# Two transpose banks shared in rotation, and every third weight load moved to SyncE's queue, in an eight-core attention and ternary-FFN kernel

## The chip, the cores and the metric

One Trainium2 chip, all eight NeuronCores. Each core runs the same program on one of the eight sequences of the batch, and no core waits for another. The metric is the device time of the slowest core in microseconds (us). The engines are called PE (TensorE, matmuls), DVE (VectorE), ACT (ScalarE), POOL (GpSimd) and SP (SyncE, which here only issues DMAs).

## The reference

One post-norm transformer layer on x of shape (8, 2048, 2048), cut to what is computed:

```python
q, k, v = x @ Wq, x @ Wk, x @ Wv            # 32 query heads, 8 key/value heads of 64; rope on q, k
a = softmax(causal(q k^T / 8)) v            # heads joined again
x = layernorm(x + a @ Wo)                   # no affine part
def weight_quant(w):                        # ternary: one scale for the whole matrix
    s = 1 / clip(mean(abs(w)), 1e-5); return clip(round(w * s), -1, 1) / s
def bitlinear(x, w):                        # w: (out, in)
    return quant8(rmsnorm(x)) @ weight_quant(w).T
h = silu(bitlinear(x, w_gate)) * bitlinear(x, w_up)       # hidden 8192
x = layernorm(x + bitlinear(h, w_down))
```

The biases are zero but added. `mean(abs(w))` needs one pass over each of the three weight matrices (64 MB each in fp32) before any of them can be quantised.

## The kernel before, in words

The program is written as a list of steps. `S.add(engine, channel, key, fn, deps)` appends a step to one engine's program; the order of the calls is the order on that engine, and a step waits (on semaphores) for every step in `deps`. An engine runs its steps strictly in that order. A DMA step belongs to the engine whose queue issues it, and its wait holds up whatever stands behind it on that engine. Each channel has one semaphore and belongs to one engine. `Rot` hands out buffers in rotation: `next()` gives the slot, the buffer and what last used it (`fr`), `used()` records who must be done before the slot comes round again.

The stages, in order:

- **x and its transposes** (0 to 358 us). For each of 16 token tiles `m`: SP loads x (1 MB, two buffers, `axl`), ACT casts it to bf16 (`axc`, L299), PE transposes it into psX, four blocks of 128 columns at a time, and DVE copies each out (`axe`, L315; 4 of them). Then 8 **pieces** of the weight-mean pass.
- **The weight-mean pass**, `pp_piece`. 384 pieces of 128x1024 fp32 (512 KB). A piece is a load (`ppl`, L285) into one of three buffers `pp_stg`, issued by ACT, and a sum of absolute values on DVE (`ppa`, L287). 128 pieces stand in the first stage, 8 for each m; 256 stand in the attention stage, 4 for each head pair. Piece `idx` uses slot `idx % 3`.
- **q, k, v** (to 1256 us). Weights come in 256 KB pieces through SP (`awl`, L328) and are cast by ACT (L332).
- **Attention** (to about 4500 us). Four query blocks g of 512, in each 16 head pairs p. For a pair: scores on PE and exp on ACT for all key tiles (`bexp`, L542), then the four pieces (their loads stand on ACT's queue behind the pair's last exp, their sums on DVE in front of the pair's `bave`), then for both heads: psAV (L560), its copy av_s (`bave`, L569), transposes, the division and the copy into attn_fm. PE starts the next pair's scores only after that, so exp waits for the whole chain. Then the output projection with 2 MB slabs through SP, and the norms.
- **FFN part 1** (about 4500 to 8640 us). First the activations come back and are transposed: 16 tiles, in each two groups of eight 128x128 transposes (`fxt`, L828) into **one** PSUM bank psTT, each copied out by DVE (`fxe`, L835). Then 64 blocks `ht` of 128 hidden rows. In a block DVE quantises the gate rows to ternary (terng, L855 to L858) and the up rows (ternu, L864 to L867). PE transposes each in two groups of eight (`ftt`, L879) through the same psTT, and DVE copies each group out (`fte`, L886) to wgT or wuT. Then for n = 0..3: 16 matmuls gate (L893), 16 matmuls up (L916), DVE's products, a max and a min, and a small matmul of the squares (L944). At the end of the block DVE quantises 128x2048 of w_down (L969 to L972), PE transposes it in two groups through another single bank psTD (`fdt`, L981), DVE copies both out (`fde`, L988), and POOL stores them.
- **FFN part 2** (to the end): int8 activations, the down projection, the last norm. Nothing in it is touched.

The chains that keep one bank from being overwritten are two variables: `last_tt` holds the last copy out of psTT and `last_fde` that out of psTD, and each next group of transposes depends on it.

DVE's order in a block is: terng, ternu, copy g0, copy g1, copy u0, copy u1, then the products of n = 0..3, then ternd, copy d0, copy d1. PE's is: transposes g0, g1, u0, u1, the matmuls of n = 0..3, transposes d0, d1.

Of the kernel before, what the change touches and what calls it, by code (L numbers as in the profile page):

```python
# [9 lines left out]
BF16 = mybir.dt.bfloat16  # L10
# [141 lines left out]
def build(nc, debug=(), upto="ALL"):  # L152
# [40 lines left out]
    S = Sched(nc, top)  # L193
# [79 lines left out]
    def pp_piece(idx):  # L273
# [10 lines left out]
        S.add("scalar", pp_stg.ch(sl), ("ppl", idx),  # L284
# [126 lines left out]
    for i in range(64):  # L411
        r, c = divmod(i, 4)
# [345 lines left out]
    psTT = ps(fst, "psTT", [128, 1024], BF16)  # L758
    psTD = ps(fst, "psTD", [128, 1024], BF16)
# [57 lines left out]
    last_tt = [None]  # L817
    xq_sp_done = [S.last("d_xqs0"), S.last("d_xqs1")]
    for m in range(NT):
# [5 lines left out]
        for j in range(2):  # L825
            def xtf(e, b=buf, j=j):
                for c in range(8 * j, 8 * j + 8):
                    i = e.transpose(psTT[:, (c % 8) * 128:(c % 8 + 1) * 128],  # L828
                                    b[:, c * 128:(c + 1) * 128], identb[:])
                return i  # L830
            S.add("tensor", "mm", ("fxt", m, j), xtf, deps=[("fxl", m), last_tt[0]])
            def xte(e, m=m, j=j):
                dst = xqT[:].rearrange("p (f t) -> p f t", f=ND)[:, 8 * j:8 * j + 8,
                                                                m * 128:(m + 1) * 128]
                return e.tensor_copy(dst, psTT[:].rearrange("p (s c) -> p s c", s=8))  # L835
            S.add("vector", "ve", ("fxe", m, j), xte, deps=[("fxt", m, j)])
            last_tt[0] = ("fxe", m, j)
# [4 lines left out]
    last_fde = [None]  # L842
    for ht in range(NFH):
# [30 lines left out]
        for nm, tern, dstT, dfr, qkey in (("g", terng, gT, gTfr, ("fgq", ht)),  # L874
                                          ("u", ternu, uT, uTfr, ("fuq", ht))):
            for j in range(2):
                def ttf2(e, tern=tern, j=j):
                    for c in range(8 * j, 8 * j + 8):
                        i = e.transpose(psTT[:, (c % 8) * 128:(c % 8 + 1) * 128],  # L879
# [3 lines left out]
                      deps=[qkey, last_tt[0]] + (dfr if j == 0 else []))  # L883
                def tte(e, dstT=dstT, j=j):
                    dst = dstT[:].rearrange("p (f c) -> p f c", f=ND)[:, 8 * j:8 * j + 8, :]
                    return e.tensor_copy(dst, psTT[:].rearrange("p (s c) -> p s c", s=8))  # L886
                S.add("vector", "ve", ("fte", nm, ht, j), tte, deps=[("ftt", nm, ht, j)])
                last_tt[0] = ("fte", nm, ht, j)
# [89 lines left out]
        for j in range(2):  # L978
            def dtf(e, o=tdb, j=j):
                for c in range(8 * j, 8 * j + 8):  # L980
                    i = e.transpose(psTD[:, (c % 8) * 128:(c % 8 + 1) * 128],  # L981
# [3 lines left out]
                  deps=[("fdq", ht), last_fde[0]] + (wtfr if j == 0 else []))  # L985
            def dte(e, wtb=wtb, j=j):
                dst = wtb[:].rearrange("p (c q) -> p c q", c=ND)[:, 8 * j:8 * j + 8, :]
                return e.tensor_copy(dst, psTD[:].rearrange("p (s c) -> p s c", s=8))  # L988
            S.add("vector", "ve", ("fde", ht, j), dte, deps=[("fdt", ht, j)])
            last_fde[0] = ("fde", ht, j)  # L990
# [12 lines left out]
    for n in range(4):  # L1003
        po = (n % 2) * 64
        for c in range(4):
            idx = n * 4 + c
            S.add("tensor", "mm", ("fstt", idx),
                  lambda e, po=po, n=n, c=c, idx=idx: e.transpose(
                      psTT[:, (idx % 8) * 128:(idx % 8) * 128 + 64],
                      stp[po:po + 64, (n // 2) * 512 + c * 128:(n // 2) * 512 + (c + 1) * 128],  # L1010
                      identb[po:po + 64, po:po + 64]),
                  deps=[("fsv",), ("fstr", idx - 1) if idx >= 1 else None,
# [265 lines left out]
```

How the kernel before makes its waits and increments, by code:

```python
    def bar(self, e, inst):  # L82
        ch = self._cur_ch
        self.ecnt[ch] = self.ecnt.get(ch, 0) + 1
        inst.then_inc(self.sem(ch), 1)
        e.wait_ge(self.sem(ch), self.ecnt[ch])
# [17 lines left out]
            def body(eng):  # L104
                waited = {}
                for s in engsteps:
                    own = ENGCH.get(s.eng)
                    ownv = self.ecnt.get(own, 0) if own is not None else 0
                    if own is not None and ownv > waited.get(own, -1):
                        eng.wait_ge(self.sem(own), ownv)
                        waited[own] = ownv
                    for d in s.deps:
                        ch, v, peng = table[d]
                        if waited.get(ch, -1) >= v:
                            continue
                        eng.wait_ge(self.sem(ch), v)
                        waited[ch] = v
                    self._cur_ch = s.ch
                    inst = s.fn(eng)
                    inst.then_inc(self.sem(s.ch), s.inc)
                    self.ecnt[s.ch] = self.ecnt.get(s.ch, 0) + s.inc
                    assert self.ecnt[s.ch] == table[s.key][1], \
                        f"step {s.key}: emitted {self.ecnt[s.ch]} != planned {table[s.key][1]} (nbar mismatch)"
```

## Time and profile before

| | |
|---|---|
| median of 3 runs | 11738.02 us (11729.38 to 11750.48) |
| the profiled execution | 11751.26 us, span of its slowest core (core 3) 11749.7 us |
| spans of the eight cores | 11715.5 to 11749.7 us |
| mean granted TensorE clock | 0.701 to 0.706 of full speed |
| busy: PE / DVE / ACT / POOL | 5747.7 / 4763.7 / 1243.3 / 955.1 us |
| idle time of DVE before L287, ended by a landing pp_stg load | w_down 851.6, w_up 477.3, w_gate 111.9 us |

Busy time is a mean over stages with different limits. PE is busy for 49% of the span, DVE for 41%, so neither is the bound throughout: what sets the time in each stage is a chain that goes from one engine to the other and back. The text after the number in square brackets on a row of the timeline says what ended the idle time before that instruction.

### The profile page before, as it was taken

What the parts mean: (1) busy time and instruction counts of PE and PEld (TensorE: products, weight loads), DVE (VectorE), ACT (ScalarE), POOL (GpSimd) and SP (SyncE); (2) the same over time, 40 slices, a digit from 0 to 9 for tenths busy, and PEclk for the clock granted to TensorE, in tenths of its full rate; (3) what the DMA queues carried; (4) which work ended last, traced back from release to release, by engine and by line L of the source; (5) the groups of instructions that cost most, each with busy time, mean ns of one, the idle gap of its engine ahead of it and who ended that gap; (6) DMA issues with size and microseconds to landing.
All of it is one profiled execution on the core that took longest, in us unless ns stands there. A gap on an engine that the chain in (4) does not pass through costs nothing. (4 is left out here: it accounts for less than half of the span.)

```text
span 11749.7 us, 84716 instructions; the slowest of 8 cores (11715.5 to 11749.7 us)
## 1 busy us (share of the span) xinstructions
PE 5747.7 (49%) x27032; PEld 2847.2 (24%) x27032; DVE 4763.7 (41%) x6288; ACT 1243.3 (11%) x2029; POOL 955.1 (8%) x1158
## 2 busy tenths in 40 slices
PE   1463243545545663656656666665630455303554
PEld 0221111111111121222222222222210344202443
DVE  5440234242242125444444444444445333464333
ACT  0101111213313420000000000000000000000000
POOL 0000110101100100000000000000013000031000
PEclk9876555565565565777777877877765778656877
DMA  7423231121121122222222222222212111122111
GB/s 237 138 82 88 80 97 61 65 83 54 50 84 46 43 77 74 79 79 75 74 79 80 68 79 79 73 75 79 76 49 72 49 52 37 64 73 60 38 51 50
DMA packets 394188, 865.55 MB, mean 74 GB/s; under 512 B 33140, under 2 KB 234004, under 8 KB 363030
## 3 DMA queue, kind: packets, MB, share of 16 engines
q1 hardware_dynamic: 286424, 482.57, 13.2%
q10 hardware_dynamic: 64512, 218.13, 5.9%
q0 software_dynamic: 42816, 159.43, 4.0%
q8 instruction: 225, 3.69, 0.1%
q14 instruction: 211, 1.73, 0.1%
HBM read 700.62 MB, written 159.40 MB: 73 GB/s over the span
## 5 line engine op out<-in xcount | busy, mean ns | idle before, releaser
L1164 PE MATMUL psD<-wdts,xcol 128*128 128x256 bf16 x8192 | 1152.3, 313 | 1841.7 <-DVE xcol L1155 1603.8
L1164 PEld LDWEIGHTS psD<-wdts,xcol 128*128 128x128 bf16 x8192 | 908.2, 112 | 2087.1 <-issue 1875.2
L893 PE MATMUL psG<-xqT,wgT 128*128 128x512 bf16 x4096 | 1105.0, 431 | 0.0
L287 DVE TENSOR_REDUCE ppart<-pp_stg 128x1 f32<-128x1024 f32 x384 | 468.5, 1220 | 1471.6 <-DMA pp_stg<-w_down 851.6
L916 PE MATMUL psU<-xqT,wuT 128*128 128x512 bf16 x4096 | 925.8, 379 | 0.0
L528 PE MATMUL psS<-qT,kT 64*128 64x512 bf16 x1280 | 653.8, 578 | 200.8 <-ACT pA L542 109.3
L1178 DVE SCALAR_TENSOR_TENSOR z2h<-psD,c3col,x2c 128x256 bf16<-128x256 f32 x128 | 61.9, 484 | 1357.5 <-PE psD L1164 1357.5
L901 DVE TENSOR_TENSOR gtr<-psG,gbc 128x512 f32<-128x512 f32 x256 | 177.0, 692 | 1004.3 <-PE psG L893 1004.3
L893 PEld LDWEIGHTS psG<-xqT,wgT 128*128 128x128 bf16 x4096 | 429.0, 109 | 600.8 <-issue 277.9
L1155 DVE CAST xcol<-xq2res 128x8192 bf16<-128x8192 int8 x128 | 566.7, 4427 | 13.6 <-DVE z2h L1178 0.5
L542 ACT ACTIVATE pA<-psS 128x512 bf16<-128x512 f32 x640 | 382.1, 597 | 1443.8 <-PE psS L528 1356.1
L916 PEld LDWEIGHTS psU<-xqT,wuT 128*128 128x128 bf16 x4096 | 400.8, 98 | 483.3
L352 PE MATMUL psQ<-wslab,xT 128*128 128x512 bf16 x1536 | 420.9, 447 | 184.9 <-ACT wslab L332 184.9
L906 ACT ACTIVATE gsil<-gtr 128x512 f32<-128x512 f32 x256 | 161.1, 629 | 2886.3 <-DVE gtr L901 2886.3
L879 PE MATMUL psTT<-identb,terng 128*128 128x128 bf16 x1024 | 129.5, 307 | 602.8 <-DVE terng L858 362.6
L952 POOL DMA_DIRECT2D h_spill<-h2c x256 | 139.1, 543 | 3281.6 <-DVE h2c L924 3167.8
L542 ACT ACTIVATE pB<-psS 128x512 bf16<-128x512 f32 x640 | 382.2, 597 | 96.5 <-ACT pA L542 3.8
L1128 POOL TENSOR_TENSOR tq<-h2rl,cbc 128x1024 f32<-128x1024 f32 x128 | 299.3, 2338 | 656.1 <-DVE xq2res L1139 622.7
L560 PE MATMUL psAV<-pA,v_buf 128*65 128x512 bf16 x640 | 256.2, 578 | 176.2 <-POOL pA L547 176.2
L574 PE MATMUL psW<-identf,av_s 65*128 65x65 f32 x512 | 77.0, 296 | 538.7 <-DVE av_s L569 538.7
L944 PE MATMUL psST<-sqc,onesb 128*64 128x512 bf16 x256 | 96.5, 377 | 475.6 <-ACT sqc L940 475.6
L547 POOL TENSOR_SCALAR_AFFINE_SELECT pA<-pA 128x512 bf16<-128x512 bf16 x256 | 156.7, 612 | 2059.4 <-ACT pA L542 2022.6
(178 smaller groups left out, 6371.4 us busy)
## 6 DMA issues: line engine op xcount, KB each, us to landing
pp_stg<-w_gate ACTq DMA_DIRECT2D x128, 512.0 KB, 5.6
pp_stg<-w_up ACTq DMA_DIRECT2D x128, 512.0 KB, 4.8
pp_stg<-w_down ACTq DMA_DIRECT2D x128, 512.0 KB, 4.6
wgst<-w_gate SPq DMA_DIRECT2D x64, 1024.0 KB, 5.0
wust<-w_up SPq DMA_DIRECT2D x64, 1024.0 KB, 4.8
wdst<-w_down SPq DMA_DIRECT2D x64, 1024.0 KB, 4.8
h_spill<-h2c POOLq DMA_DIRECT2D x256, 256.0 KB, 2.6
h2rl<-h_spill SPq DMA_DIRECT2D x128, 512.0 KB, 3.6
```

Of the source, the lines that this page charges most:

```text
L287: lambda e, b=buf, idx=idx: e.tensor_reduce(ppart[:, idx:idx + 1], b[:], AX.X, OP.add, apply_absolute_value=True),
L352: i = e.matmul(p_[:], xT[:, kc * T + m * 128:kc * T + (m + 1) * 128], w[:, kc * 512:(kc + 1) * 512], start=(kc == 0), stop=(kc == 15))
L528: lambda e, kv=kv, kt=kt, p=p, poff=poff, bank=bank: e.matmul(psS[bank][:], kT[poff:poff + 64, kv * T + kt * 128:kv * T + (kt + 1) * 128], ...
L542: lambda e, pb=pX[X], kt=kt, bank=bank: e.activation(pb[:, kt * 512:(kt + 1) * 512], psS[bank][:], AF.Exp),
L560: i = e.matmul(psAV[0:65, :], v_buf[:, kt * 520 + hv * 65:kt * 520 + hv * 65 + 65], pb[:, kt * 512:(kt + 1) * 512], start=(kt == 0), stop= ...
L893: i = e.matmul(p_[:], gT[:, kc * 128:(kc + 1) * 128], xqT[:, kc * T + n * 512:kc * T + n * 512 + 512], start=(kc == 0), stop=(kc == 15))
L901: lambda e, p_=gps, n=n: e.tensor_tensor(gtr[:], p_[:], gbc[:, n * 512:(n + 1) * 512], OP.mult),
L906: lambda e, o=gsb3: e.activation(o[:], gtr[:], AF.Silu),
L916: i = e.matmul(p_[:], uT[:, kc * 128:(kc + 1) * 128], xqT[:, kc * T + n * 512:kc * T + n * 512 + 512], start=(kc == 0), stop=(kc == 15))
L1128: lambda e, b=buf, o=tb, hf=hf: e.tensor_tensor(o[:], b[:], cbc[:, hf * 1024:(hf + 1) * 1024], OP.mult),
L1155: lambda e, o=cb4, m=m: e.tensor_copy(o[:].rearrange("p (k c) -> p k c", k=NFH), xq2res[:].rearrange("p (k c) -> p k c", k=NFH)[:, :, m * ...
L1164: i = e.matmul(p_[0:128, 0:256], c_[:, hk * 128:(hk + 1) * 128], w[:, hk * 256:(hk + 1) * 256], start=(hk == 0), stop=(hk == NFH - 1))
```

## The change

Two things. In the weight-mean pass, the loads of slot 1 are issued by SP in place of ACT (one in three). In FFN part 1, psTT and psTD become one rotation psTX of two banks, and every group of eight transposes (xq, gate, up, down, and the 16 small ones of the sums of squares) takes the next bank and waits only for the copy that last read that bank. The number of PSUM banks, the transposes, the copies and the order on each engine stay as they are, except for the moved loads.

```diff
         sl, buf, fr = pp_stg.next()
-        S.add("scalar", pp_stg.ch(sl), ("ppl", idx),
+        S.add("scalar" if sl != 1 else "sync", pp_stg.ch(sl), ("ppl", idx),
               lambda e, b=buf, s=src: e.dma_start(out=b[:], in_=s), deps=[fr], dma=True)
...
-    psTT = ps(fst, "psTT", [128, 1024], BF16)
-    psTD = ps(fst, "psTD", [128, 1024], BF16)
+    psTX = Rot([ps(fst, f"psTX{i}", [128, 1024], BF16) for i in range(2)], "psTX")
...
         for j in range(2):
-            def xtf(e, b=buf, j=j):
+            tsl, tbuf, tfr = psTX.next()
+            def xtf(e, b=buf, j=j, tb=tbuf):
...
-            S.add("tensor", "mm", ("fxt", m, j), xtf, deps=[("fxl", m), last_tt[0]])
+            S.add("tensor", "mm", ("fxt", m, j), xtf, deps=[("fxl", m)] + tfr)
...
             S.add("vector", "ve", ("fxe", m, j), xte, deps=[("fxt", m, j)])
-            last_tt[0] = ("fxe", m, j)
+            psTX.used(tsl, ("fxe", m, j))
...
                 S.add("tensor", "mm", ("ftt", nm, ht, j), ttf2,
-                      deps=[qkey, last_tt[0]] + (dfr if j == 0 else []))
+                      deps=[qkey] + tfr + (dfr if j == 0 else []))
...
                 S.add("vector", "ve", ("fte", nm, ht, j), tte, deps=[("ftt", nm, ht, j)])
-                last_tt[0] = ("fte", nm, ht, j)
+                psTX.used(tsl, ("fte", nm, ht, j))
...
             S.add("tensor", "mm", ("fdt", ht, j), dtf,
-                  deps=[("fdq", ht), last_fde[0]] + (wtfr if j == 0 else []))
+                  deps=[("fdq", ht)] + tfr + (wtfr if j == 0 else []))
...
             S.add("vector", "ve", ("fde", ht, j), dte, deps=[("fdt", ht, j)])
-            last_fde[0] = ("fde", ht, j)
+            psTX.used(tsl, ("fde", ht, j))
...
-                  deps=[("fsv",), ("fstr", idx - 1) if idx >= 1 else None,
-                        ("fte", "u", NFH - 1, 1)])
+                  deps=[("fsv",), ("fte", "u", NFH - 1, 1)] + tfr)
```

## Rows read from the trace of the kernel before

**Rows 1.** Stretches: time, busy PE, PEld, DVE, ACT, POOL, PEclk, DMA, GB/s.

```profile
1256.00:4500.00 3244.00, 1592.79 (x5024) 542.56 (x5024) 1055.91 (x2315) 780.68 (x1318) 328.85 (x541) 0.58 0.20 66
4640.00:8640.00 4000.00, 2448.28 (x11524) 1151.69 (x11524) 1919.20 (x2246) 323.69 (x513) 245.46 (x320) 0.79 0.23 75
```

**Rows 2.** Timeline, one FFN block, gate and up weights: start, duration, instruction, idle before.

```profile
6451.81 1.23 DVE L858 TENSOR_TENSOR terng<-pq_b,qq_b 128x2048 bf16<-128x2048 bf16 x1
...
6453.28 1.01 PE L879 MATMUL psTT<-identb,terng 128*128 128x128 bf16 x8 [5.62 <-DVE terng L858]
...
6457.19 0.69 DVE L886 COPY wgT<-psTT 128x1024 bf16<-128x1024 bf16 x1 [0.17 <-DVE ternu L867]
6458.03 1.01 PE L879 MATMUL psTT<-identb,terng 128*128 128x128 bf16 x8 [3.73 <-DVE wgT L886]
6459.14 0.69 DVE L886 COPY wgT<-psTT 128x1024 bf16<-128x1024 bf16 x1 [1.26 <-PE psTT L879]
6460.09 1.01 PE L879 MATMUL psTT<-identb,ternu 128*128 128x128 bf16 x8 [1.05 <-DVE wgT L886]
...
6462.04 1.01 PE L879 MATMUL psTT<-identb,ternu 128*128 128x128 bf16 x8 [0.94 <-DVE wuT L886]
6462.85 4.92 PE L893 MATMUL psG<-xqT,wgT 128*128 128x512 bf16 x16
...
6512.69 1.22 DVE L858 TENSOR_TENSOR terng<-pq_b,qq_b 128x2048 bf16<-128x2048 bf16 x1
```

**Rows 3.** Timeline, the same block's w_down transposes.

```profile
6444.69 1.01 PE L981 MATMUL psTD<-identb,ternd 128*128 128x128 bf16 x8 [4.42 <-DVE ternd L972]
6445.81 0.69 DVE L988 COPY wdtst<-psTD 128x1024 bf16<-128x1024 bf16 x1 [1.37 <-PE psTD L981]
6446.65 1.01 PE L981 MATMUL psTD<-identb,ternd 128*128 128x128 bf16 x8 [0.94 <-DVE wdtst L988]
6447.76 0.69 DVE L988 COPY wdtst<-psTD 128x1024 bf16<-128x1024 bf16 x1 [1.26 <-PE psTD L981]
```

**Rows 4.** Instructions of tile terng: count, duration min/median/max ns, first and last start.

```profile
L858 DVE TENSOR_TENSOR terng<-pq_b,qq_b x64: 1224/1225/1227, 4644.7 to 8576.1; 128x2048 bf16<-128x2048 bf16 x64
```

**Rows 5.** Stretches of one or a few us inside FFN blocks, columns as in rows 1.

```profile
6462.80:6465.20 2.40, 2.40 (x9) 0.93 (x7) 0.69 (x1) 0.00 (x0) 0.00 (x0) 0.50 0.00 0
...
6421.00:6424.50 3.50, 3.50 (x10) 1.23 (x9) 0.00 (x0) 0.00 (x0) 0.00 (x0) 0.52 0.01 4
```

**Rows 6.** Timeline, gate matmuls of two successive n in one block.

```profile
6410.76 3.63 PE L893 MATMUL psG<-xqT,wgT 128*128 128x512 bf16 x16
...
6420.05 5.31 PE L893 MATMUL psG<-xqT,wgT 128*128 128x512 bf16 x16
```

**Rows 7.** Timeline, one of the 32 xq transpose groups.

```profile
4580.62 1.01 PE L828 MATMUL psTT<-identb,xqrl 128*128 128x128 bf16 x8 [0.94 <-DVE xqT L835]
```

**Rows 8.** Tile xqrl: landing times of its 16 loads.

```profile
DMA to landing us min/median/max: 3.3/3.8/12.6
```

**Rows 9.** Timeline, attention, one head pair whose first piece is in slot 1.

```profile
1404.54 5.78 ACTq L285 DMA_DIRECT2D pp_stg<-w_up  x4
...
1408.68 1.22 DVE L287 TENSOR_REDUCE ppart<-pp_stg 128x1 f32<-128x1024 f32 x1 [10.19 <-DMA pp_stg<-w_up]
...
1414.13 1.22 DVE L287 TENSOR_REDUCE ppart<-pp_stg 128x1 f32<-128x1024 f32 x1 [1.44 <-DMA pp_stg<-w_up]
1415.52 0.69 DVE L569 COPY av_s<-psAV 65x512 f32<-65x512 f32 x1 [0.17 <-DVE ppart L287]
```

**Rows 10.** Timeline, first stage, end of tile m = 9 and start of m = 10.

```profile
228.56 1.22 DVE L287 TENSOR_REDUCE ppart<-pp_stg 128x1 f32<-128x1024 f32 x1 [0.17 <-DVE ppart L287]
...
230.35 1.91 ACT L299 ACTIVATE xbf<-x_stage 128x2048 bf16<-128x2048 f32 x1 [20.58 <-DVE ppart L287]
...
237.34 0.42 DVE L315 COPY xT<-psX 128x512 bf16<-128x512 bf16 x1 [0.17 <-DVE ppart L287]
```

**Rows 11.** Tile x_stage: landing times of its 16 loads.

```profile
DMA to landing us min/median/max: 7.0/8.1/10.0
```

More of the change, by code:

```diff
@@ L876, in build, with ttf2 @@
             for j in range(2):
-                def ttf2(e, tern=tern, j=j):
+                tsl, tbuf, tfr = psTX.next()
+                def ttf2(e, tern=tern, j=j, tb=tbuf):
                     for c in range(8 * j, 8 * j + 8):
-                        i = e.transpose(psTT[:, (c % 8) * 128:(c % 8 + 1) * 128],
+                        i = e.transpose(tb[:, (c % 8) * 128:(c % 8 + 1) * 128],
                                         tern[:, c * 128:(c + 1) * 128], identb[:])
@@ L978, in build, with dtf @@
         for j in range(2):
-            def dtf(e, o=tdb, j=j):
+            tsl, tbuf, tfr = psTX.next()
+            def dtf(e, o=tdb, j=j, tb=tbuf):
                 for c in range(8 * j, 8 * j + 8):
-                    i = e.transpose(psTD[:, (c % 8) * 128:(c % 8 + 1) * 128],
+                    i = e.transpose(tb[:, (c % 8) * 128:(c % 8 + 1) * 128],
                                     o[:, c * 128:(c + 1) * 128], identb[:])
@@ L1006, in build @@
             idx = n * 4 + c
+            tsl, tbuf, tfr = psTX.next()
             S.add("tensor", "mm", ("fstt", idx),
-                  lambda e, po=po, n=n, c=c, idx=idx: e.transpose(
-                      psTT[:, (idx % 8) * 128:(idx % 8) * 128 + 64],
+                  lambda e, po=po, n=n, c=c, tb=tbuf: e.transpose(
+                      tb[:, 0:64],
                       stp[po:po + 64, (n // 2) * 512 + c * 128:(n // 2) * 512 + (c + 1) * 128],
                       identb[po:po + 64, po:po + 64]),
-                  deps=[("fsv",), ("fstr", idx - 1) if idx >= 1 else None,
-                        ("fte", "u", NFH - 1, 1)])
+                  deps=[("fsv",), ("fte", "u", NFH - 1, 1)] + tfr)
             S.add("vector", "ve", ("fstr", idx),
-                  lambda e, idx=idx: e.tensor_reduce(
-                      ftm[:, idx:idx + 1], psTT[:, (idx % 8) * 128:(idx % 8) * 128 + 64],
+                  lambda e, idx=idx, tb=tbuf: e.tensor_reduce(
+                      ftm[:, idx:idx + 1], tb[:, 0:64],
                       AX.X, OP.add),
                   deps=[("fstt", idx)])
+            psTX.used(tsl, ("fstr", idx))
     fam_last = [("famP", NFH - 1, 3), ("famN", NFH - 1, 3)]
```

16 lines of the change are left out of this document (7 added, 9 removed).

## The prediction, as it went on record

> **What bounds the kernel now.** I read the list of stretches first, to see which stages the change touches and what they are worth. FFN part 1 takes 4000 us from 4640 on, with PE busy 2448 of them and DVE 1919; the attention stage takes 3244 us with PE busy 1593, DVE 1056 and ACT 781 [rows 1]. No engine is full in either, so a chain from engine to engine sets the time, and the timeline has to say which.
>
> In an FFN block the timeline [rows 2] shows where PE is idle before the matmuls. The gate rows are ternary at 6453.04 and the first gate matmul starts at 6462.85, 9.81 us later. In between PE works 4 times 1.01 us. It waits for ternu, because DVE makes ternu before it copies out the first group; then each group waits for the copy of the one before, and each copy for its group. DVE is idle 1.26 us before each of the copies after the first. Here the two engines take turns in one bank. The same turn-taking stands at the end of the block [rows 3], and there it is DVE's own chain: the next block's terng is queued behind the second wdtst copy. The block lasts 60.88 us from terng to terng [rows 2]; over all 64 the mean is (8576.1 - 4644.7)/63 = 62.40 us [rows 4].
>
> In the attention stage the four sums of a head pair stand in front of av_s on DVE. Their loads are issued behind the pair's last exp: from the first issue to av_s it is 10.98 us in the pair shown [rows 9]. Everything behind av_s, up to the next pair's exp, waits. In the first stage the last of each tile's loads holds ACT's cast of the next x tile, which is then already in its buffer [rows 10].
>
> **The change part by part, FFN.** Nothing is added to an engine; two waits for a bank go away in each pair of groups. The rotation is g0, g1, u0, u1, d0, d1 in banks 0, 1, 0, 1, 0, 1, so a group waits for the copy two places earlier. For g0 and d0 these copies are long done.
>
> *Gate and up.* g0 runs at 6453.28 as before and g1 directly behind it, both under ternu. DVE copies g0 at 6457.19 to 6457.88 as before, then g1 at 6458.05 to 6458.74 (0.17 between DVE steps, as in front of the copy at 6457.19). PE's u0 can start 0.15 after the first copy, at 6458.03, where g1 stood. u1 follows it: behind eight transposes at 0.81 us a group (6462.04 to 6462.85), but not before 6458.74 + 0.15 = 6458.89. The gate matmuls start at 6458.89 + 0.81 = 6459.70 in place of 6462.85, which is 3.15 us earlier. The copies of u0 and u1 end near 6460.8, under the gate matmuls, before the up matmuls need them.
>
> *Down.* d1 follows d0 at 6445.50 and ends at 6446.51; the second copy starts at 6446.50 + 0.17 = 6446.67 and ends at 6447.36 in place of 6448.45, 1.09 us earlier, and terng of the next block moves with it.
>
> Sum: 4.24 us a block, 64 blocks: 271 us. Between the two places PE's and DVE's matmul part is unchanged.
>
> *Clock.* The first part of the gate matmuls runs at 0.50, which is 1.2 GHz [rows 5], so they take 4.92 us [rows 2] against 3.63 [rows 6]. PE's unbroken work begins at 6462.04, 0.81 us before the gate matmuls; after the change it begins at 6458.03, 1.67 us before them. If the clock rises as long after its beginning as now, 0.86 us less of the matmuls is at half speed, 0.43 us a block, 27 us in all; if it doesn't, nothing. I take 20. The clock also falls inside some blocks: 0.52 over 3.5 us [rows 5], which makes 16 matmuls 5.31 us long instead of 3.63, 1.68 more [rows 6]. Such stretches, and the varying first part, are what lifts the mean block over the shown one: 62.40 - 60.88 = 1.52 us, 97 us over 64 blocks. Where they fall depends on how the block's pattern lies in time, which the change shifts. They may all go (97 gained) or double (97 lost). I take zero, as the part of the block in which they fall is unchanged.
>
> *xq transposes.* A group takes 1.01 + 0.94 = 1.95 us [rows 7]; with two banks each bank is reused after 1.95, so 0.98 a group, 31 us over 32 groups. But both groups of a tile wait for its load, and there are two load buffers: a buffer's load can't be issued before its tile is transposed and lands 3.3 to 3.8 us later [rows 8], so a tile takes 3.4 to 3.9 us after the change against 3.91 now. That leaves 0 to 8 us. With the 16 small transposes at the end I take 5 and keep 0 to 35.
>
> FFN in all: 271 + 20 + 5 = 296 us.
>
> **Attention.** The loads of slot 1 now stand on SP, which in the pairs has nothing else to issue. So slot 1 is filled again as soon as DVE has summed it, long before the pair's last exp. Four pieces on three slots: a pair starts in slot 2, 0 or 1 in turn. In pairs that start in slot 2 or 0 the fourth piece takes the slot of the first; ACT still issues that load only when the first is landed and summed, and av_s stays where it is: gain 0. In pairs that start in slot 1 both slot-1 pieces are already there and summed or landed, ACT issues two loads in place of four, and nothing is issued late. The first landed sum starts 4.14 us after the issue (1408.68 - 1404.54); three sums at 1.39 apart (1415.52 - 1414.13) end the wait at 4.14 + 3 x 1.39 = 8.31 in place of 10.98 [rows 9], a gain of 2.67. I take 2.4, since not every pair waits as long for the fourth load. There are 21 such pairs of 64: 50 us. Bounds: 0 (the loads contend with each other) and 21 x 2.67 with some more where slabs of Wo delay the fourth load, 75.
>
> This is where a page speaks against the change. The trace shows loads of 512 KB whose first sum comes 4.14 us after the issue, whatever the queue is [rows 9]. The Trainium skill, page "DMA: Bandwidth & Descriptors", section "Issuing engines are not separate DMA queues", says that queues of several engines run on the same 16 DMA engines, and that using several saves only the sequencers' time to issue. By that rule the 50 us would be 0. I think that the rule doesn't reach this case, since what is saved is the wait behind exp and not bandwidth.
>
> **First stage.** Here SP isn't free: it loads x. The load of tile m+1 stood ahead, waiting only for a cast that is long done; now it stands behind the slot-1 pieces of tile m, each of which waits for a sum on DVE. Nothing in this stage hides it: DVE's copies of tile m+1 wait for PE, PE for the cast, the cast for x.
>
> - Tiles with slots 0 1 2 0 1 2 0 1 (m = 0, 3, ..., 15): the eighth piece waits for the fifth sum, 229.78 in tile 9 [rows 10]. x is issued at about 230.3 and lands 8.1 us later [rows 11], 238.4; the cast of 1.91 is done at 240.3, and with some 1 us for PE's transposes (a group of eight takes 1.01 [rows 7]) the first copy comes at 241.3 (now the cast could let it come at 233.3, and the sums hold it until 237.34). Late by 3.9 us, five times before the last tile: 20.
> - Tiles with 1 2 0 1 2 0 1 2: the seventh piece waits for the fourth sum, 1.39 us earlier: late by 2.5, five times: 12.
> - Tiles with 2 0 1 ...: the sixth waits for the third sum, early enough for the cast; but 1 MB then moves while DVE waits for its own pieces. I take 1, five times: 5.
> - After the last tile the first Wq pieces, also prefetched by SP now, are issued late: 3, once.
>
> Loss 40 us. With landing at 7.0 and no contention it would be about 20, and 10 if prefetched slot 1 pieces give something back; with 10.0 at each of the 15 tiles 5.8 x 15 = 87.
>
> **Sum.** -296 - 50 + 40 = -306 us. The profiled execution took 11751.26 us, so 11445; the median of the runs shown is 13 us below the profiled one, so 11432 us.
>
> **The rivals.**
>
> *A, the clock takes part of the gain back.* If the half-speed stretches of 3.5 us come in most blocks and the earlier rise doesn't, FFN gives 271 - 97 + 5 = 179 us and the time is 11549. Half of that effect gives about 11500. For it: the clock does fall inside blocks now. Against: the matmul part keeps its pattern.
>
> *B, the lost prefetch of x costs more.* 87 in place of 40: 11479.
>
> *C, attention gains nothing*, as the queue rule has it: 11482.
>
> *D, the FFN gain isn't there, because a second bank doesn't shorten a chain that something else holds.* Then -50 + 40 = -10: 11728, no change that can be told. Against it stand all four idle times in [rows 2] and two in [rows 3], which name the copy or the transposes and nothing else. The Trainium skill, page "TensorE: Matmul & The Clock Gate", section "HAM oscillation — how this bites in real kernels", tells of a kernel in which double-buffering PSUM gave no further gain; by that FFN would give nothing. That kernel waited for loads, and here the rows name no load.
>
> *E, slower.* One mechanism: PE works more densely, and the clock falls in nearly every n of the 256. Each fall costs 1.68 us [rows 6]. To eat 306 us it needs 182 more falls than now; if every n had one more, 430 us would be lost and the time is 11862. For it: only that the falls exist; against: the density inside n is unchanged.
>
> *F, the clock gives more*: the falls go away, and 97 us with them: 11335.
>
> **How the numbers follow.** The forecast has 0.68, A 0.10, B 0.07, C 0.06, F 0.05, D 0.02, E 0.02. The range reaches from 11345 (most of F, with the attention and first-stage terms at their better ends) to 11510 (B and C, half of A). What lies outside is the rest of A and F, D and E, near 0.15. A measurement of this kernel can tell about 0.2%, 23 us, from no change. Only D lies within it and only E above: faster 0.95, same 0.03, slower 0.02.
>
> **What would show it.** In the changed profile: the time from the end of terng to the first gate matmul 6.66 us in place of 9.81; no idle of 0.94 us between transpose groups; 2.67 us from the first w_down transposes to the second wdtst copy's end in place of 3.76; mean block near 57.9. In attention: every third pair with two loads on ACT's queue and av_s 8.2 us after the first issue, the others at 10.4 to 11. In the first stage: the cast waits for x in place of a sum, and the stage ends near 395 in place of 358. FFN part 2 unchanged. The prediction is wrong if FFN blocks get shorter by less than 3 us (the clock), if the pairs of the other two kinds move, or if the first stage doesn't grow.

## The result, and the profile after

The changed kernel takes 11429.53 us (median of 8 runs, 11405.74 to 11447.54), the kernel before 11740.51 (8 runs on the same chip, 11729.38 to 11751.99). The ratio is 0.9735, with a 95% interval of 0.9724 to 0.9745. The forecast was 11432. The profiled execution took 11437.69 us, with a span of 11436.0 on core 3, which is also the core shown of before.

This table lays core 3's two spans side by side, cut at the instructions named. The 5.1 us between the last xq transpose and the first terng stand in no row and are the same in both:

| stretch | before | after | change | predicted |
|---|---|---|---|---|
| start to the end of the 128th L287 | 365.6 | 404.4 | +38.8 | +37 |
| to the first q matmul | 25.3 | 29.2 | +3.9 | +3 |
| q, k, v, to the first score | 869.6 | 875.6 | +6.0 | 0 |
| attention, first score to last av_s | 3074.2 | 3015.9 | -58.3 | -50 |
| to the first xq transpose | 242.0 | 242.1 | +0.1 | 0 |
| xq transposes | 62.9 | 47.3 | -15.6 | -5, with the small ones |
| 63 blocks, terng to terng | 3931.4 | 3654.2 | -277.2 | -286 |
| the last block | 60.3 | 55.6 | -4.7 | -4.6 |
| small transposes and the rest up to psD | 539.1 | 534.2 | -4.9 | in the -5 |
| FFN part 2 | 2574.1 | 2572.3 | -1.8 | 0 |

The changes add up to -313.7 us, for a forecast of -306. The page's row of the sums of absolute values has 816.0 us of idle time ended by w_down's loads where the one before had 851.6:

```profile
L287 DVE TENSOR_REDUCE ppart<-pp_stg 128x1 f32<-128x1024 f32 x384 | 468.5, 1220 | 1437.9 <-DMA pp_stg<-w_down 816.0
```

**FFN part 1.** These are the two stretches that answer to [rows 1], moved to where the stages now lie; the columns are the same.

```profile
1305.00:4500.00 3195.00, 1572.59 (x5024) 536.09 (x5024) 1063.49 (x2330) 780.89 (x1319) 329.39 (x542) 0.59 0.21 67
4620.00:8330.00 3710.00, 2400.86 (x11520) 1164.03 (x11520) 1912.95 (x2239) 323.70 (x513) 244.30 (x320) 0.81 0.25 81
```

FFN part 1 needs 3710 us for the DVE work for which it needed 4000 (1912.95 us against 1919.20), so what went is DVE's idle time. The timeline of one block, from the w_down transposes of the block before to the gate matmuls, answers to [rows 2, 3]:

```profile
6643.64 1.87 PE L981 MATMUL psTX<-identb,ternd 128*128 128x128 bf16 x16 [4.42 <-DVE ternd L971]
6644.76 0.69 DVE L988 COPY wdtst<-psTX 128x1024 bf16<-128x1024 bf16 x1 [1.37 <-PE psTX L981]
6645.62 0.69 DVE L988 COPY wdtst<-psTX 128x1024 bf16<-128x1024 bf16 x1 [0.17 <-PE psTX L981]
...
6649.66 1.23 DVE L856 TENSOR_TENSOR terng<-pq_b,qq_b 128x2048 bf16<-128x2048 bf16 x1
...
6651.14 1.86 PE L878 MATMUL psTX<-identb,terng 128*128 128x128 bf16 x16 [5.64 <-DVE terng L856]
...
6655.05 0.69 DVE L885 COPY wgT<-psTX 128x1024 bf16<-128x1024 bf16 x1 [0.17 <-DVE ternu L865]
6655.91 0.69 DVE L885 COPY wgT<-psTX 128x1024 bf16<-128x1024 bf16 x1 [0.17 <-DVE wgT L885]
...
6655.99 1.87 PE L878 MATMUL psTX<-identb,ternu 128*128 128x128 bf16 x16 [2.98 <-DVE wgT L885]
6657.10 0.69 DVE L885 COPY wuT<-psTX 128x1024 bf16<-128x1024 bf16 x1 [0.51 <-PE psTX L878]
...
6657.65 5.15 PE L892 MATMUL psG<-xqT,wgT 128*128 128x512 bf16 x16
```

Sixteen transposes now stand in one row where there were two groups of eight with 0.94 idle between them. From terng's end (6650.89) to the first gate matmul it is 6.76 us. In the w_down part, first transposes to the end of the second copy (6646.31) is 2.67 us. All 64 blocks are in the row of terng, which answers to [rows 4]: the mean block is (8273.9 - 4619.6)/63 = 58.00 us.

```profile
L856 DVE TENSOR_TENSOR terng<-pq_b,qq_b x64: 1224/1225/1227, 4619.6 to 8273.9; 128x2048 bf16<-128x2048 bf16 x64
```

The clock still falls inside blocks, as in [rows 5, 6]. Here are PE instructions of the same block, the second and the third gate row, each behind a small matmul (L943). The stretch below them lies in the third gate row and has the granted clock 0.52:

```profile
6668.05 0.38 PE L943 MATMUL psST<-sqc,onesb 128*64 128x512 bf16 x1 [1.79 <-ACT sqc L939]
6668.35 3.63 PE L892 MATMUL psG<-xqT,wgT 128*128 128x512 bf16 x16
...
6677.34 0.38 PE L943 MATMUL psST<-sqc,onesb 128*64 128x512 bf16 x1 [1.90 <-ACT sqc L939]
6677.65 5.31 PE L892 MATMUL psG<-xqT,wgT 128*128 128x512 bf16 x16
```

```profile
6677.90:6681.40 3.50, 3.50 (x10) 1.31 (x9) 0.00 (x0) 0.00 (x0) 0.00 (x0) 0.52 0.22 80
```

**Attention.** A pair that starts in slot 1, in the timeline (answers to [rows 9]):

```profile
3976.15 0.82 ACTq L285 DMA_DIRECT2D pp_stg<-w_down  x2
...
3980.16 1.22 DVE L287 TENSOR_REDUCE ppart<-pp_stg 128x1 f32<-128x1024 f32 x1 [26.30 <-DMA pp_stg<-w_down]
3981.55 1.22 DVE L287 TENSOR_REDUCE ppart<-pp_stg 128x1 f32<-128x1024 f32 x1 [0.17 <-DVE ppart L287]
3982.95 1.22 DVE L287 TENSOR_REDUCE ppart<-pp_stg 128x1 f32<-128x1024 f32 x1 [0.17 <-DVE ppart L287]
3984.24 0.33 SPq L285 DMA_DIRECT2D pp_stg<-w_down  x1
3984.34 0.69 DVE L569 COPY av_s<-psAV 65x512 f32<-65x512 f32 x1 [0.17 <-DVE ppart L287]
```

ACT issues two loads and av_s starts 8.19 us after the first. The prediction says of these loads' time that it is the same "whatever the queue is", for which [rows 9], with ACT's loads alone, was no evidence. The changed kernel has it: a load that SP issues with no other piece in flight lands after 3.67 us (median of 362 in all cores), and one that it issues some 1.4 us behind one of ACT's after 4.70. In the kernel with all loads on ACT's queue further down (*the middle key tile*) the same two figures are 3.69 and 4.70.

**First stage.** The end of tile m = 9 and the start of m = 10 (answers to [rows 10]), and the landing times of x_stage ([rows 11]):

```profile
251.39 0.38 SPq L295 DMA_DIRECT2D x_stage<-x  x1
...
258.18 0.33 SPq L285 DMA_DIRECT2D pp_stg<-w_gate  x1
259.29 1.91 ACT L299 ACTIVATE xbf<-x_stage 128x2048 bf16<-128x2048 f32 x1 [23.58 <-DMA x_stage<-x]
...
262.14 0.42 DVE L315 COPY xT<-psX 128x512 bf16<-128x512 bf16 x1 [4.04 <-PE psX L307]
```

```profile
DMA to landing us min/median/max: 6.2/8.1/11.2
```

ACT's cast is now released by x itself, where a sum released it before, and DVE is idle for 4.04 us in front of the first copy. The forecast had 3.9 us late for such a tile. Tiles 1, 4, 7, 10 and 13 have 4.1 to 4.4 us of it (means of the cores), tiles 3, 6, 9, 12 and 15 have 0.8 to 1.0, and the others 0.2, as every tile had before.

### The profile page after: what moved, and what is told of

Read it like the earlier page. It is cut to its first block and busy times, and to the rows that moved or that the text cites. A ratio compares the mean times of both kernels' runs of the same rounds, so it can differ in the third digit from the quotient of the medians.

```text
span 11436.0 us, 84644 instructions; the slowest of 8 cores (11383.3 to 11436.0 us)
## 1 busy us (share of the span) xinstructions
PE 5682.2 (50%) x27032; PEld 2855.3 (25%) x27032; DVE 4763.7 (42%) x6288; ACT 1243.3 (11%) x2029; POOL 955.1 (8%) x1158
## 3 DMA queue, kind: packets, MB, share of 16 engines
q8 instruction: 225, 3.69, 0.1%
## 5 line engine op out<-in xcount | busy, mean ns | idle before, releaser
L287 DVE TENSOR_REDUCE ppart<-pp_stg 128x1 f32<-128x1024 f32 x384 | 468.5, 1220 | 1437.9 <-DMA pp_stg<-w_down 816.0
L943 PE MATMUL psST<-sqc,onesb 128*64 128x512 bf16 x256 | 96.9, 379 | 475.5 <-ACT sqc L939 475.5
L923 DVE TENSOR_TENSOR h2c<-psU,gsil 128x512 f32<-128x512 f32 x256 | 177.1, 692 | 319.4 <-PE psU L915 319.2
```

The costliest lines, as they stand in the source:

```text
L287: lambda e, b=buf, idx=idx: e.tensor_reduce(ppart[:, idx:idx + 1], b[:], AX.X, OP.add, apply_absolute_value=True),
L923: lambda e, p_=ups, o=h2b, g_=gsb3: e.tensor_tensor(o[:], p_[:], g_[:], OP.mult),
```

## The experiments

Each batch had its own runs of the kernel before; their medians were 11765.41 (first batch), 11774.21 (second) and 11741.65 us (third). Stage and block times are those of core 3 unless a range over cores is given.

Totals are compared by their ratios, and with one more caution. The total is that of the slowest core, and in all runs but one some cores have stretches at a granted clock of 0.81 in FFN part 1 (last section), not the same ones each time. In *slot 1 early* core 5, the slowest, had 532 us of it there and a mean block of 59.34 us, where the cores without it had 58.0: 83 us in the total that the edit didn't make. In *banks only* core 7 had 309 us and 58.78, which is 48. So the readings below go by stages, and by the blocks of cores that had little or none of it.

### The two halves apart

*Banks only*: the rotation of two banks, all piece loads on ACT.

```diff
-        S.add("scalar" if sl != 1 else "sync", pp_stg.ch(sl), ("ppl", idx),
+        S.add("scalar", pp_stg.ch(sl), ("ppl", idx),
```

> The two banks in rotation, with all weight loads issued by ACT as in the kernel before. Theory: the shift in the FFN stage and nothing else, 277 us in the 63 blocks between the first and the last terng, 5 in the last block, 16 in the xq transposes, 5 in the small transposes at the end: about 304 us under the kernel before, so near 11437 us, a ratio of 0.974. The stage up to the last L287 of the 128th piece ends at 365.6 as before, and attention (first scores to last av_s) takes 3074 us as before. Rival 1: the moved loads carry part of the gain, in that the FFN stage gains less without them; then the 63 blocks keep more than 3700 us. Rival 2: a second bank gives nothing; ratio 1.00.

Measured 11488.57 us, ratio 0.975 (0.9707 to 0.9793); the expected 11437 lacks the 48 us at 0.81. First stage 365.1, attention 3068.8, mean block 58.02.

*Queue only*: the kernel before, with slot 1's loads on SP (the same line the other way round).

> Only the slot-1 loads moved to SP, psTT and psTD as in the kernel before. Theory: first stage 39 us longer, first Wq pieces and the q, k, v stage up to 10 us longer, attention 58 us shorter: a net of -10 to -20 us, 11720 to 11730 us, a ratio of 0.998 to 0.999. Blocks at 62.40 us. Rival (queues of several engines share the same DMA engines, so that nothing is gained by a second queue): attention stays at 3074 us and the kernel is 40 us slower, ratio 1.003.

Measured 11747.84 us, ratio 0.9979 (0.9958 to 0.9999). First stage 403.1, attention 3000.9, mean block 62.42.

The halves don't touch each other: each has its own stages' times of the changed kernel and the other half's times of before. The banks make all of the FFN gain. The queue alone is worth about 25 us by its ratio, with an interval of 1 to 49: some 70 gained in attention, some 40 lost in the first stage and 6 more up to the first q matmul.

### Was the loss in the first stage x's place behind the pieces?

*x ahead*: SP loads tile m+1 before it comes to tile m's pieces.

```diff
+    x_next = x_load(0)
     for m in range(NT):
+        sl, buf = x_next
+        if m + 1 < NT:
+            x_next = x_load(m + 1)
```

> The changed kernel, with x tile m+1 issued on SP's queue before tile m's slot-1 pieces. Theory (x lost its place in the queue): first stage back from 404 us to about 366, Wq pieces still late by up to 4, total about 11391 us, a ratio of 0.970 to the kernel before. Rival (x and a third of the pieces now share SP's rings and slow each other down, whatever the order): first stage stays above 390 and the total at 11430. Second rival: with x ahead and a second queue, the pieces themselves come earlier, first stage under 355.

Measured 11431.07 us, ratio 0.9705 (0.9671 to 0.974). That is 40 us above the expected 11391. On the slowest core 31 of them are blocks at 0.81 (217 us of it, mean block 58.49). The first stage lasts 362 to 383 us over the cores, against 396 to 405. This is the timeline of its m = 9 to 10:

```profile
240.69 1.91 ACT L305 ACTIVATE xbf<-x_stage 128x2048 bf16<-128x2048 f32 x1 [22.16 <-DVE ppart L287]
242.00 0.38 SPq L295 DMA_DIRECT2D x_stage<-x  x1
...
250.07 0.42 DVE L321 COPY xT<-psX 128x512 bf16<-128x512 bf16 x1 [0.17 <-DVE ppart L287]
```

The cast's releaser is a sum again, and DVE goes from its last sum straight to the copy. The mean of the cores is 371.6 us here, 402.5 in *queue only* and 368.2 in *banks only*, all of this batch: 31 of 34 us come back. What was lost has two parts. DVE's idle time in front of the copies of x was 43.0 us before, 66.5 in the changed kernel and is 43.0 again. Its idle time in front of the sums was 116.5 us before, 134.0 in the changed kernel, and is 127.9 here against 124.6 in *banks only*. The first Wq pieces stay late: the stretch to the first q matmul was 32 to 39 us here, 25 to 28 in *banks only*.

### Is it the queue, or the place in the order?

The queue rule of the prediction's rival C says that another queue gives nothing. These two keep every load on ACT and move only where slot 1's loads stand in ACT's order: the first one ahead of the pair's exps, and a pair's second one (if it has two) ahead of the last key tile's exps, or of the middle one's.

```diff
+                if kt == 0:
+                    pp_piece(ones[0], add=False)
+                if kt == nkt - 1 and len(ones) == 2:
+                    pp_piece(ones[1], add=False)
```

The other kernel has `kt == nkt // 2` in place of `kt == nkt - 1`. The first to run was the one with the last key tile (*slot 1 early*):

> All piece loads on ACT, but in attention the slot-1 loads stand ahead of the pair's exps (the second one of a pair, where there are two, ahead of the last key tile's exps). No second queue. Theory (the place in the program's order, not the queue): attention as in the changed kernel, about 3000 us against 3070 before, first stage as before, about 360, total near 11390. Rival (a second queue is what helps): attention stays at 3060 to 3075 as with the banks alone.

Measured 11481.45 us, ratio 0.9748 (0.9694 to 0.9802); attention 3033 to 3060 us over the cores. The mean of the cores is 3044, against 3067 before and 2996 in the changed kernel, so two thirds of the expected gain are missing. The timeline of a slot-1 pair, whose last exp starts at 3944.01 and takes 0.60:

```profile
3942.83 0.34 ACTq L287 DMA_DIRECT2D pp_stg<-w_down  x1
...
3950.11 1.22 DVE L291 TENSOR_REDUCE ppart<-pp_stg 128x1 f32<-128x1024 f32 x1 [28.09 <-DMA pp_stg<-w_down]
...
3954.29 0.69 DVE L578 COPY av_s<-psAV 65x512 f32<-65x512 f32 x1 [0.17 <-DVE ppart L291]
```

ACT issues its two other loads at 3944.96, and the first sum starts 5.15 us later instead of 4.01 (3980.16 - 3976.15 in the changed kernel). The first of these two lands after 5.42 us (median over such pairs and all cores), where it takes 3.88 in the changed kernel. The load issued 2.1 us ahead of it is then still on its way. So the place in the order isn't all that counts: a load issued while another is on its way lands later, here as above (4.70 us against 3.67).

With the middle key tile in place of the last:

> As the run with slot-1 loads early on ACT, but the second slot-1 load of a pair stands ahead of the exps of the middle key tile in place of the last. In that run the load issued 1.8 us before the last exp's end moved while ACT's own two loads were in flight, and these landed at 5.4 to 6.2 us in place of 3.8 to 4.1. Theory (place and contention, not the queue): pairs that start in slot 1 reach av_s 8.0 to 8.9 us after the last exp in query blocks 1 to 3, as with SP, and attention on core 3 takes 3000 to 3025 us. Rival (a second queue is what helps): these pairs stay at 9.7 us or more and attention at 3045 and above.

Measured 11386.73 us, ratio 0.9702 (0.9681 to 0.9723); attention 2989 to 3004 us. A slot-1 pair in its timeline:

```profile
3886.27 8.50 ACTq L287 DMA_DIRECT2D pp_stg<-w_down  x3
...
3890.35 1.22 DVE L291 TENSOR_REDUCE ppart<-pp_stg 128x1 f32<-128x1024 f32 x1 [27.02 <-DMA pp_stg<-w_down]
...
3894.53 0.69 DVE L578 COPY av_s<-psAV 65x512 f32<-65x512 f32 x1 [0.17 <-DVE ppart L291]
```

First issue to av_s is 8.26 us, as on SP. The first of ACT's two late loads lands after 3.90 us. So the whole attention gain can be had on one queue. The rule of the Trainium skill (page "DMA: Bandwidth & Descriptors", section "Issuing engines are not separate DMA queues"), that a second issuing engine saves only the time to issue, holds here: 2989 to 3004 us with one queue against 2983 to 3016 with two. What paid was to take a load out from behind the exps. And since SP is left alone, x keeps its prefetch: the first stage is back at 352 to 367 us.

*All of attention's pieces on SP*, the first stage's all on ACT: the same idea taken to its end.

```diff
-        S.add("scalar" if sl != 1 else "sync", pp_stg.ch(sl), ("ppl", idx),
+        S.add("scalar" if idx < 128 else "sync",
+              pp_stg.ch(sl) if idx < 128 else f"d_pq{sl}", ("ppl", idx),
```

> The changed banks; the first stage's piece loads all on ACT, the attention stage's all on SP (three slots). Theory (what costs is that a load stands behind the pair's last exp, and in the first stage that x stands behind pieces): first stage back at 355 to 375 us. In attention all four pieces of a pair are loaded and summed during its exps, so av_s starts when PE has finished psAV, 2.2, 4.0, 5.0 and 6.2 us after the last exp in the four query blocks in place of 10.4: (8.2 + 6.4 + 5.4 + 4.2) x 16 = 387 us under the kernel before, so attention near 2685 us and the total near 11060. Rival (the loads' own bandwidth or latency sets the pace, whatever the place of the issue): attention stays above 2900.

Measured 11046.82 us, ratio 0.9384 (0.9337 to 0.9431); attention 2615 to 2649 us over the cores. DVE in one pair of core 4:

```profile
2503.16 1.22 DVE L287 TENSOR_REDUCE ppart<-pp_stg 128x1 f32<-128x1024 f32 x1 [0.17 <-DVE ppart L287]
2506.32 1.22 DVE L287 TENSOR_REDUCE ppart<-pp_stg 128x1 f32<-128x1024 f32 x1 [1.93 <-DMA pp_stg<-w_down]
2523.81 0.69 DVE L569 COPY av_s<-psAV 65x512 f32<-65x512 f32 x1 [16.27 <-PE psAV L560]
```

All sums are done during the pair's exps, and av_s waits for its own matmuls. From the last exp's end to av_s it is 2.5, 4.2, 5.2 and 6.5 us in the four query blocks (medians), against 8.2 to 11.6 in the changed kernel.

### Does the clock take part of the FFN gain back?

*Down in turns*: d1 waits for the copy of d0 again, so 1.09 us a block should come back.

```diff
-                  deps=[("fdq", ht)] + tfr + (wtfr if j == 0 else []))
+                  deps=[("fdq", ht)] + tfr + (wtfr if j == 0 else [("fde", ht, 0)]))
```

> The changed kernel, where the second group of w_down transposes of a block waits again for the copy of the first. Theory: each block loses the 1.09 us that this place was worth, 64 x 1.09 = 70 us: about 11500 us, mean block 59.1 in place of 58.00. Rival: DVE's chain there is bound by something else (the clock, the copies themselves), and the wait costs less than 0.5 us a block, under 11465. Rival 2: the clock's pattern answers to the shift by more than the step itself, and the mean block comes out outside 58.8 to 59.4.

Measured 11459.45 us, ratio 0.9736 (0.9701 to 0.977). The wait is there (PE in its timeline), and yet the mean block is (8227.8 - 4562.0)/63 = 58.19 us, 0.19 above the changed kernel's:

```profile
6647.21 1.01 PE L981 MATMUL psTX<-identb,ternd 128*128 128x128 bf16 x8 [4.39 <-DVE ternd L971]
6649.17 1.01 PE L981 MATMUL psTX<-identb,ternd 128*128 128x128 bf16 x8 [0.94 <-DVE wdtst L988]
```

```profile
L856 DVE TENSOR_TENSOR terng<-pq_b,qq_b x64: 1224/1225/1226, 4562.0 to 8227.8; 128x2048 bf16<-128x2048 bf16 x64
```

I counted the gate and up matmuls of all blocks of core 3 that start 0.43 us after the one before instead of 0.22, which is what a 512-column matmul takes at 1.2 and at 2.4 GHz in these traces. (Core 3 has a record of all 128 of a block. Two cores of each run lack three, and a gap in the records looks like a slow matmul.) In the changed kernel they are 7.1 a block at its beginning and 4.9 later, and the clock falls inside 37 of 63 blocks. With d in turns they are 5.6 and 2.0, and it falls inside 15 to 18. These are 4.4 fewer, each 0.213 us: 0.94 us. So 1.09 were added, 0.94 paid back, which leaves 0.15. The same short waits stood in every block of both kernels, only placed 1.09 us apart; why that makes the falls rarer isn't shown. All eight cores have it, and yet the program alone doesn't fix the count: in the kernel with the middle key tile, whose FFN is the changed kernel's, three cores had 27, 28 and 34.

*Squares late*: the small matmul of the squares (L943), for which PE waits 1.8 to 1.9 us while the gate matmuls behind it could run, stands behind the next n's gate matmuls, for n = 0 to 2.

```diff
         for n in range(4):
...
             S.add("tensor", "mm", ("fgm", ht, n), gmm, ...)
+            if n:
+                late_fsm()
...
-            S.add("tensor", "mm", ("fsm", ht, n), ...)
+            if n == 3:
+                fsm()
+            else:
+                late_fsm = fsm
```

> The changed kernel, with the small matmul of the squares (L944) of n = 0, 1, 2 issued on PE behind the gate matmuls of n + 1. PE no longer idles 1.8 to 1.9 us for ACT's squares in three of four n. Theory of the clock: the clock falls inside a block because of these repeated idle stretches; without them it falls inside at most a tenth of the blocks in place of 37 of 63. Mean block: 58.0 - 3 x 1.8 = 52.6 with the falls as they are, 51.5 without them; total near 11030. Rival (denser work makes the clock fall more often): more than 4.9 matmuls a block at half speed behind the first part, mean block above 53.5.

Measured 11057.53 us, ratio 0.9384 (0.9332 to 0.9437). The clock falls inside none of the 63 blocks, and the mean block is (7845.7 - 4620.2)/63 = 51.20 us. PE in one n:

```profile
6032.88 3.62 PE L892 MATMUL psG<-xqT,wgT 128*128 128x512 bf16 x16
6036.43 0.40 PE L946 MATMUL psST<-sqc,onesb 128*64 128x512 bf16 x1
6036.76 3.63 PE L917 MATMUL psU<-xqT,wuT 128*128 128x512 bf16 x16
```

```profile
L856 DVE TENSOR_TENSOR terng<-pq_b,qq_b x64: 1224/1225/1227, 4620.2 to 7845.7; 128x2048 bf16<-128x2048 bf16 x64
```

Of the 6.80 us a block, three waits of 1.8 to 1.9 us are 5.5; the 4.9 later slow matmuls that are gone are 1.04, and 0.8 fewer at the beginning 0.17. So it was those waits that let the clock fall.

*The same with d in turns*: where there are no falls to take away, the 1.09 us should stay lost.

> The kernel with the squares late (no falls of the clock inside blocks), and the second group of w_down transposes waiting again for the first one's copy. Theory (with the changed kernel the same wait cost only 0.2 us a block, since the clock fell inside 16 blocks in place of 37 and gave back the rest): with no falls to give back, the wait costs its 1.09 us, mean block 52.3 on the cores where it was 51.2, total near 11125. Rival (the wait itself costs little, because the copies on DVE are bound elsewhere): mean block under 51.6.

Measured 11057.96 us, ratio 0.9424 (0.9396 to 0.9452). The mean block is (7852.9 - 4567.4)/63 = 52.15 us, 0.95 above 51.20; the slow matmuls at the beginning went from 6.3 to 5.8, which pays back 0.1. The totals alone could not tell: their ratios are 0.9384 and 0.9424, with intervals that overlap, and the slowest cores had blocks at 0.81 in both runs.

*Filled waits*: the changed kernel with 22 and 10 more matmuls of 128x512 in PE's two long waits of a block, whose results nobody reads.

```diff
+        def keep(key, count, deps):
+            def f(e):
+                for _ in range(count):
+                    i = e.matmul(psG.bufs[0][:], identb[:], xqT[:, 0:512],
+                                 start=True, stop=True)
+                return i
+            S.add("tensor", "mm", key, f, deps=deps)
+        if ht:
+            keep(("kp1", ht), 22, [("fgs", ht - 1, 2)])
...
+            if nm == "u" and ht:
+                keep(("kp2", ht), 10, [])
```

The 22 stand ahead of the gate transposes, the 10 ahead of the up transposes.

> The changed kernel with work that is thrown away: 22 matmuls of 128x512 on PE between a block's w_down transposes and the next block's gate transposes, and 10 between the gate and the up transposes, where PE idles 5.6 and 2.9 us. Theory (the first gate matmuls run at 1.2 GHz since PE idles ahead of them): the 7.1 matmuls a block at half speed go, the gate matmuls of n = 0 take 3.6 us, and the mean block falls by 7.1 x 0.21 = 1.5 us to 56.5: total near 11335. If the falls inside the blocks go too, 55.5 and 11270. Rival (the added matmuls delay the transposes or the clock falls through higher load): mean block 58 or more.

Measured 11351.26 us, ratio 0.9643 (0.9595 to 0.9692). PE in its timeline:

```profile
6614.69 5.52 PE L873 MATMUL psG<-xqT,identb 128*128 128x512 bf16 x22
...
6625.39 0.61 PE L889 MATMUL psTX<-identb,ternu 128*128 128x128 bf16 x8 [1.63 <-DVE wgT L896]
...
6626.59 3.62 PE L903 MATMUL psG<-xqT,wgT 128*128 128x512 bf16 x16
```

The first gate row takes 3.62 us where it took 5.15, and eight transposes 0.61 us where they took 1.01. The mean block falls from 58.00 to 56.84. Two parts make it up (means of the 63 blocks): from the first gate matmul to the first up matmul 4.94 us became 4.17, 0.77 less, and from terng's end to the first gate matmul 6.78 became 6.37, 0.41 less, as the transposes run at the full clock too. The falls inside remain (38 to 46 blocks). In this run the q, k, v stage was also shorter on cores 0 to 3, 821 to 823 us against 850 to 854 on the cores of before that had no granted clock of 0.81 there (see the last section). Its instructions are the same. The difference stands in one place: ACT waits for the 64 pieces of Wo for 205 to 210 us in all, against 227 to 230 before, and these loads land after a median of 2.97 to 3.01 us in place of 3.26 to 3.36 on all eight cores. Why they land sooner is open.

### The pieces together

*Attention's pieces on SP, and squares late:*

> The squares late, and the attention loads all on SP with the first stage's all on ACT. The stages don't touch each other, so the gains add: attention near 2635, blocks at 51.2 to 52.3, first stage 350 to 366: 11047 - 372 = 10675 us, a ratio of 0.907 to 0.910 to the kernel before. Rival (denser work makes the chip grant less clock in the FFN): blocks above 53 on more than two cores and a total above 10740.

Measured 10581.52 us, ratio 0.902 (0.8998 to 0.9041): attention 2616 to 2633 us over the cores, mean block 51.21.

*The same with filled waits:*

> As the run with both, with the thrown-away matmuls (22 and 10 a block) in PE's waits. Gain theory: the 6.3 matmuls at half speed at a block's start fall to about 2, 0.9 us a block, 58 us in all: 10620. Rival (the granted clock falls below full for longer, as cores 4 to 7 showed 0.81 for 807 to 1048 us with the filled waits alone): the stretches at 0.81 exceed 1000 us on some cores, the gate and up matmuls there take 20 percent longer, and the total is 10675 or more.

Measured 10489.41 us, ratio 0.8953 (0.8922 to 0.8984), the fastest kernel of the study. The mean block is 50.38 us in place of 51.21. From the first gate matmul to the first up matmul it is 4.38 us in place of 4.81, and from terng's end to the first gate matmul 6.39 in place of 6.80: 0.43 and 0.41 make up the 0.83. Of the 92 us against the kernel without fillers 52 are the blocks' (63 x 0.83). The q, k, v stage gives some 28 more, and again ACT's wait for Wo's pieces is shorter (204 to 206 us against 226 to 234, landing after 2.95 to 2.98 us against 3.22 to 3.34).

## Why the prediction was right, point by point

The total is closer than its parts. The forecast of 11432 is 2.5 us off, while single terms are off by 9 (the blocks), 8 (attention), 16 (xq and small transposes) and 6 (q, k, v), and most of it cancels: the sum is -313.7 in place of -306, and the median lies 8 us below the profiled run in place of 13. That last closeness is luck.

- **Gate and up: right.** terng's end to the first gate matmul went from 9.82 to 6.76 us, where 6.66 was predicted: 3.06 of the 3.15 us. u1 follows u0 with no wait, since the second wgT copy ends at 6656.60, before u0's eight transposes are through. The missing 0.10: PE starts u0 0.25 us after the first copy's end (6655.74 to 6655.99), and I took 0.15.
- **Down: right.** 3.76 to 2.67 us, as predicted.
- **Clock at the block's beginning: right.** 8.5 slow matmuls became 7.1, 0.30 us a block; 0.31 had been taken.
- **Clock inside the blocks (rival A): right for this kernel.** It falls inside 37 blocks where it fell inside 36. But the reason given, that the matmul part's pattern is unchanged, is weaker than I made it. In the experiment with d in turns the pattern was just as unchanged, and the falls went from 37 blocks to 15 to 18. That the count stayed was partly luck: the kernel could have come out some 40 us (0.62 us x 63 blocks) faster.
- **xq and small transposes: mis-sized.** -15.6 and -4.9 us in place of -5 in all. The step that failed is "a tile takes 3.4 to 3.9 us after the change": the landing (median 3.7 us now, as in [rows 8]) comes once for each two tiles, since two buffers are on their way together. With a tile's two groups of 0.98 us (1.95, [rows 7]) that gives (3.7 + 1.95)/2 = 2.8 us a tile, and the stage took 47.3/16 = 2.96. The whole is inside the bound of 35.
- **Attention: right in kind.** Every third pair went from 10.45 to 10.95 us (last exp to av_s, medians of the four query blocks) to 8.2 to 8.9; the other two kinds stayed at 10.5 to 11.6. Pair by pair, the 21 pairs of the first kind give 53 us in the mean of the cores for a forecast of 50. The whole stage went from 3067 to 2996 in the mean of the cores, which is 70 (58 on core 3). Of the other 17 us, 6 lie behind av_s in the same 21 pairs, on the way to the next pair's exp, which the forecast took as unchanged. Another 9 lie in the other 43 pairs, 0.2 us each; there the cores range from 7 lost to 23 gained, so this part may be chance. Rival C is refuted as a forecast, though its rule is right: the queue isn't what gave the gain.
- **First stage: right in size and in cause, but the size partly by luck.** +38.8 and +3.9 us for 37 and 3, and the *x ahead* kernel shows that it is x's place on SP. But the forecast had two kinds of tile late by 3.9 and 2.5 us, five times each, which is 32, and the copies of x wait 4.0 and 0.7 us longer than before: 23.5 in the mean of the cores. The step that failed is "late by 2.5", where the seventh piece waits for the fourth sum. What filled the gap is the waits in front of the sums, 17.5 us longer (16 on core 3), for which the forecast had 5.
- **q, k, v: not predicted.** +6.0 us on core 3. It lies within what the cores of one run differ by, and goes with 223 us at a granted clock of 0.81 in place of 205 (last section).
- **Rivals B, D, E and F**: the loss of B did not come (42.7 us, not 87); *banks only* has the whole FFN gain, against D; and the falls neither rose as E has it nor went away as F has it. For D the prediction says of the kernel that the Trainium skill tells of (page "TensorE: Matmul & The Clock Gate", section "HAM oscillation — how this bites in real kernels") that it waited for loads; the page says so of its first form, and the second bank was added after its loop had been reordered.

## What to carry to other kernels

When two engines take turns in one buffer, the gain of a second one can be read off the timeline as the idle times that name the copy, minus what the next chain imposes; sum it by block, as here (4.24 predicted, 3.06 + 1.09 = 4.15 measured, and 0.30 for the clock). Before a load is moved to an idle queue, ask what else that queue prefetches, and whether an earlier place in the old queue gives the same: here it did, and lost nothing. After a change to a dense PE loop, count matmuls at half speed as well as the block time, since their number can hide a step of nearly 1 us, and look for short repeated waits of PE in front of a small matmul, which here cost 5.5 us a block themselves and 1.04 through the clock.

## What the runs showed of the hardware

**A third clock level, by pairs of cores.** Besides 0.5 and 1 the granted clock stands at 0.81 in stretches of 1 to 68 us (medians of 7 to 17), before and after and in every experiment but *down in turns*. A stretch of *squares late* on core 0 (columns as in [rows 1]), and a gate row of the timeline in it:

```profile
5431.00:5464.00 33.00, 30.76 (x113) 11.97 (x113) 13.82 (x20) 5.04 (x8) 2.04 (x4) 0.81 0.06 24
```

```profile
5434.66 4.38 PE L892 MATMUL psG<-xqT,wgT 128*128 128x512 bf16 x16
```

Sixteen matmuls take 4.38 us in place of 3.62. In this run cores 0, 1, 6 and 7 had 412 to 430 us of it in FFN part 1 and a mean block of 52.3 us; the others had 51.2. It comes on cores 0 and 1, 2 and 3, 4 and 5, 6 and 7 together: cores 0 and 1 had it between 5391 and 5552 us, while 2 and 3 of the same die had none in the whole stage. In the q, k, v stage the cores' differences go with it: before, six cores without it take 850 to 854 us, and cores 2 and 3 with 203 and 205 us of it 874 and 870; after, 844 to 854 on the four cores without it, and 865 to 879 on the four with 165 to 223 us. The Trainium skill, page "TensorE: Matmul & The Clock Gate", section "Seeing it yourself", tells of a peak-current limiter that grants 13/16 when three or more cores of a die run dense matmuls. The level agrees with 0.81. That it takes the whole die and holds while the load lasts doesn't agree with these rows, which show pairs of cores and gaps within dense work. What turns it on was not tried.

**Short waits and the clock.** PE waits of 1.79 and 1.90 us in front of L943, with PE otherwise busy, were enough for falls inside 36 or 37 of 63 blocks, and without them there was none. The fall doesn't come at each: the same waits gave 15 to 18 blocks when 1.09 us was added to a block.
